# Blurring the three border rows on GpSimd as a stencil in the last loop of a convolution, GroupNorm and blur kernel

## The reference

```python
def _L1_conv_ref(input, kernel):
    PAD0, PAD1 = (2, 1)
    k = jnp.flip(kernel, (0, 1))
    w = jnp.broadcast_to(k[None, None], (c, 1) + k.shape)
    xp = jnp.pad(input, ((0, 0), (0, 0), (PAD0, PAD1), (PAD0, PAD1)))
    return lax.conv_general_dilated(xp, w, window_strides=(1, 1), padding='VALID', ...)
...
x = x + _L1_conv_ref(_gn(x), L1_conv_kernel)
```

## Time and profile before

| what | value |
|---|---|
| median of 3 runs | 5608.24 us (5605.93 to 5615.25) |
| profiled execution | 5612.93 us, of it a span of 5611.1 us |
| TensorE busy | 5223.0 us (93%) |
| VectorE busy | 4318.1 us (77%) |
| ScalarE busy | 3702.3 us (66%) |
| GpSimd busy | 2095.5 us (37%) |
| moved | 1729.80 MB, 308 GB/s in the mean |

### The profile page before, as it was taken

How to read it: one execution, slowest core, us unless ns; L and a number is a source line. 1 busy time by engine, 2 the same in 40 slices (tenths; PEclk the granted TensorE clock), 3 DMA queues, 4 the chain that set the end, 5 groups by cost and what they waited for, 6 DMA issues and landing times. The chain is left out here.

```text
span 5611.1 us, 67501 instructions
## 1 busy us (share of the span) xinstructions
PE 5223.0 (93%) x18280; PEld 3171.0 (57%) x18280; DVE 4318.1 (77%) x5293; ACT 3702.3 (66%) x4976; POOL 2095.5 (37%) x1393
## 2 busy tenths in 40 slices
PE   2888888899999999997699999999999999999999
PEld 1333333334555555563266666666666667667777
DVE  8555555418999999966988888888888888888833
ACT  0333333346777777756788788787887878878754
POOL 0000000017777777742333333333333333333354
PEclk9999999999999999999899999999999999999999
DMA  9999999942333333326999999999999999999986
GB/s 372 367 383 387 376 382 377 354 147 81 106 107 108 106 109 107 105 87 258 382 388 403 394 404 399 394 404 390 395 399 388 404 392 395 404 382 404 394 273 221
DMA packets 829589, 1729.80 MB, mean 308 GB/s; under 512 B 50064, under 2 KB 587152, under 8 KB 718608
## 3 DMA queue, kind: packets, MB, share of 16 engines
q1 hardware_dynamic: 485136, 1121.34, 53.8%
q10 hardware_dynamic: 344064, 604.05, 28.1%
HBM read 1050.95 MB, written 674.23 MB: 307 GB/s over the span
## 5 line engine op out<-in xcount | busy, mean ns | idle before, releaser
L1159 POOL TENSOR_TENSOR y_lo<-y_centred_tile,y_hi 128x1024 fp32r<-128x1024 f32 x512 | 1039.7, 2052 | 1721.1 <-ACT y_centred_tile L1509 1405.3
L1380 PE MATMUL blur_psum<-y_hi,band_hi 128*128 128x512 f32 x4096 | 1128.9, 417 | 8.8 <-DVE y_tile L1248 7.4
L1380 PE MATMUL blur_psum<-y_lo,band_hi 128*128 128x512 f32 x4096 | 1042.5, 396 | 7.5 <-POOL y_lo L1159 7.1
L1363 PE MATMUL conv_psum<-u_in,w_conv 128*128 128x512 f32 x2048 | 958.1, 610 | 84.2 <-DMA u_in<-u_scratch 36.1
L1380 PEld LDWEIGHTS blur_psum<-y_hi,band_hi 128*128 128x128 f32 x4096 | 765.8, 188 | 278.9 <-issue 100.6
L1380 PEld LDWEIGHTS blur_psum<-y_lo,band_hi 128*128 128x128 f32 x4096 | 769.7, 188 | 200.8 <-POOL y_lo L1159 16.5
L1220 DVE TENSOR_TENSOR pair_sums<-gelu_out,conv_psum 128x512 f32<-128x512 f32 x960 | 613.9, 683 | 308.3 <-ACT conv_psum L1471 308.0
L1248 DVE SCALAR_TENSOR_TENSOR y_tile<-blur_psum,rstd_all,y_tile 128x1024 f32<-128x1024 f32 x512 | 639.5, 1276 | 159.7 <-PE blur_psum L1380 152.2
L1471 ACT ACTIVATE gelu_out<-conv_psum,bn_shift,bn_scale 128x512 f32<-128x512 f32 x512 | 397.9, 777 | 522.0 <-PE conv_psum L1363 498.9
L1363 PEld LDWEIGHTS conv_psum<-u_in,w_conv 128*128 128x128 f32 x2048 | 393.8, 195 | 525.3 <-issue 384.2
L396 PE MATMUL z_psum<-x_resident,w_folded 128*128 128x512 f32 x1280 | 600.0, 624 | 28.0 <-ACT z_psum L425 19.1
(11 more groups left out here) (175 smaller groups left out, 5661.9 us busy)
## 6 DMA issues: line engine op xcount, KB each, us to landing
x_tile<-x SPq DMA_DIRECT2D x256, 1024.0 KB, 9.1
y_scratch<-x_tile ACTq DMA_DIRECT2D x256, 1024.0 KB, 7.7
y_tile<-y_scratch SPq DMA_DIRECT2D x512, 512.0 KB, 12.5
out<-y_tile ACTq DMA_DIRECT2D x512, 512.0 KB, 9.7
x_stream<-x SPq DMA_DIRECT2D x192, 1024.0 KB, 11.6
x_resident<-x SPq DMA_DIRECT2D x160, 1024.0 KB, 11.2
z_scratch<-z_tile ACTq DMA_DIRECT2D x256, 256.0 KB, 7.2
z_in<-z_scratch SPq DMA_DIRECT2D x256, 256.0 KB, 3.0
```

The lines of the kernel that those rows point to most:

```text
L1159: nc.gpsimd.tensor_tensor(y_lo[:, h, part, 2:2 + W], y_c[:, part, :], y_hi[:, h, part, 2:2 + W].bitcast(F32), ALU.subtract).then_inc(s_lo, 1)
L1363: nc.tensor.matmul(cv[s][:], w[:, s * C:(s + 1) * C], u_t[:, k % US, :], start=True, stop=True).then_inc(s_mm, 1)
L1380: ins = nc.tensor.matmul(bl[t][:, 2 * c:2 * c + 2, :], wt[:, kw, :], y[:, h, ch:ch + 2, kw:kw + W], start=(m == 0 and kw == 0), stop=(m == ...
```

## The change

The seam leaves TensorE and VectorE. GpSimd computes it as a stencil in fp32 from 112 partitions: 48 of them (16 channels x 3 rows) hold the left half of the columns, 48 more, from partition 64 on, the right half. Each partition gets the four rows that its output row needs, side by side in its free dimension (4 x 131), so that the row direction too is a sum along the free dimension. SP therefore issues eight loads for a quad (four rows for two column halves) and two stores, where it issued two loads and one store. ScalarE subtracts the mean in place (two instructions of 48 partitions). GpSimd then does four quarters, one behind each y_lo pair: column tap j times the window, added up, and in the last quarter the four rows are added together, scaled by the rstd, and the row itself is added. Each instruction waits for the one before it. SP's loads of a quad now wait until the stencil of the quad two before is done. The conv product no longer waits for the seam; the matrices of the seam and their products go, and the mean and rstd tables of the seam come from one product in place of two.

The diff, without the removed constants, bands and counts:

```diff
@@ SP, in load_group @@
-                    sp.wait_ge(s_sc, b * NQ - NQ + q + 1)
-                    sp.dma_start(seam_t[:, q % 2, :], yr[bass.ds(n * GRP, 16), 125:131, :]).then_inc(s_sin[q % 2], 16)
-
-                    sp.wait_ge(s_sst[q % KS], b * (16 * NQ // KS) - 16 * NQ // KS + 16 * (q // KS) + 16)
-                    sp.dma_start(keep_t[:, q % KS, :], yr[bass.ds(n * GRP, 16), 127:130, :]).then_inc(s_sin[q % 2], 16)
+                    sp.wait_ge(s_sdn, b * NQ - NQ + q + 1)
+                    for half, (to, cols) in enumerate(SEAM_PARTS):
+                        for kh in range(4):
+                            sp.dma_start(seam_t[64 * half:64 * half + 48, q % 2, kh, to],
+                                         yr[bass.ds(n * GRP, 16), 125 + kh:128 + kh, cols]).then_inc(s_sin[q % 2], 16)
@@ GpSimd @@
-                if g % QUAD == 2:
-                    pool.wait_ge(s_sc, b * NQ - NQ + g // QUAD + 3)
-                    nc.gpsimd.tensor_tensor(seam_lo[:, 2:2 + W], seam_c[:],
-                                            seam_hi[:, 2:2 + W].bitcast(F32), ALU.subtract).then_inc(s_slo, 1)
+
+            def seam_quarter(b, phase, k):
+                qq, j = divmod(k - LAG_QUARTER, QUAD)
...
+                taps = KR[0:SEAM_P, :].rearrange("p (a b) -> p a b", b=4)[:, :, j:j + 1].broadcast_to([SEAM_P, 4, SEAM_W])
+                window = y[:, :, j:j + SEAM_W]
+                if j == 0:
+                    pool.wait_ge(s_sc, 2 * at + 2)
...
+                    nc.gpsimd.tensor_tensor(seam_acc[:], window, taps, ALU.mult).then_inc(s_slk, 1)
+                    return
+                pool.wait_ge(s_slk, links + 2 * j - 1)
+                nc.gpsimd.tensor_tensor(seam_prod[:], window, taps, ALU.mult).then_inc(s_slk, 1)
+                pool.wait_ge(s_slk, links + 2 * j)
+                nc.gpsimd.tensor_tensor(seam_acc[:], seam_acc[:], seam_prod[:], ALU.add).then_inc(s_slk, 1)
+                if j < 3:
+                    return
+                pool.wait_ge(s_slk, links + 7)
+                nc.gpsimd.tensor_tensor(seam_acc[:, 0:2], seam_acc[:, 0:2], seam_acc[:, 2:4], ALU.add).then_inc(s_slk, 1)
+                pool.wait_ge(s_slk, links + 8)
+                nc.gpsimd.tensor_tensor(seam_acc[:, 0], seam_acc[:, 0], seam_acc[:, 1], ALU.add).then_inc(s_slk, 1)
...
+                nc.gpsimd.tensor_tensor(seam_o[:, slot, :], seam_acc[:, 0], scale, ALU.mult).then_inc(s_slk, 1)
+                pool.wait_ge(s_slk, links + 10)
+                nc.gpsimd.tensor_tensor(seam_o[:, slot, :], seam_o[:, slot, :], mean, ALU.subtract).then_inc(s_slk, 1)
+                pool.wait_ge(s_slk, links + 11)
+                nc.gpsimd.tensor_tensor(seam_o[:, slot, :], seam_o[:, slot, :], y[:, 2, 2:2 + SEAM_W],
+                                        ALU.add).then_inc(s_sdn, 1)
@@ TensorE @@
-                        if blurring and (k - LAG_BLUR) % QUAD == QUAD - 1:
-                            seam(b, phase, k, seam_products)
@@ VectorE @@
-                        if (k - LAG_BLUR) % QUAD == QUAD - 1:
-                            take_seam(b, k)
@@ ScalarE, in split_seam @@
-                nc.scalar.activation(seam_hi[:, 2:2 + W], seam_t[:, q % 2, :], ACT.Identity,
-                                     bias=nm_s[:, bass.ds(at, 1)]).then_inc(s_shi, 1)
-                nc.scalar.activation(seam_c[:], seam_t[:, q % 2, :], ACT.Identity,
-                                     bias=nm_s[:, bass.ds(at, 1)]).then_inc(s_sc, 1)
+                for half, (inside, _) in enumerate(SEAM_PARTS):
+                    part = seam_t[64 * half:64 * half + 48, q % 2, :, inside]
+                    nc.scalar.activation(part, part, ACT.Identity,
+                                         bias=nm_s[64 * half:64 * half + 48, bass.ds(at, 1)]).then_inc(s_sc, 1)
```

More of the change, by code:

```diff
@@ L52, in shape_constants @@
         k[:, K_TM + kh * 128:K_TM + (kh + 1) * 128] = p[:, None] - p[None, :] == kh - 2
[L53 to L59 removed]
+    for half in range(2):
+        m = np.arange(48)
+        k[:, K_SEAM + 64 * half:K_SEAM + 64 * half + 48] = p[:, None] % 16 == m[None, :] // 3
     k[:, K_QM:K_QM + C // 16] = p[:, None] // 16 == np.arange(C // 16)[None, :]
@@ L941 @@
 YS = 8
-KS = 4
+KS = 2
+SEAM_P = 112
+SEAM_W = W // 2
 AHEAD3 = 2
@@ L948 @@
 LAG_SEAM = AHEAD3 + LAG_BLUR + 3
+LAG_QUARTER = LAG_SPLIT + 2
+LINKS_SEAM = 11
 PADW = W + 4
@@ L1167, in body @@
             def body(b, phase):
-                for k in range(LAG_SPLIT if phase == END else UNITS):
+                for k in range(LAG_QUARTER if phase == END else UNITS):
                     if phase == FIRST:
@@ L1384, in blur @@
                 ins.then_inc(s_t, 1)
-            def seam(b, phase, k, products):
-                q = (k - LAG_BLUR) // QUAD
-                at = b * NQ - NQ + q
-                pe.wait_ge(s_shi, at + 1)
-                pe.wait_ge(s_slo, at + 1)
-                if phase <= MIDDLE:
-                    pe.wait_ge(s_ge, b * (4 * UNITS) + 4 * k + 3 + 4)
-                elif k == LAG_BLUR - 1 and phase == DRAIN:
-                    pe.wait_ge(s_tab, b)
-                if k != LAG_BLUR + QUAD - 1 or phase != SECOND:
-                    pe.wait_ge(s_sev, at)
-                for m, (wt, y) in enumerate(products):
-                    for kw in range(4):
-                        ins = nc.tensor.matmul(small[0:48, 0:W], wt[:, kw, :], y[:, kw:kw + W],
-                                               start=(m == 0 and kw == 0),
-                                               stop=(m == len(products) - 1 and kw == 3))
-                ins.then_inc(s_smm, 1)
             def gn2_average(b, phase):
```

120 lines of the change are left out of this document (50 added, 70 removed).

## The result

The changed kernel takes **5641.91 us** (median of 5 runs, 5626.83 to 5646.33) against 5608.24; the ratio is 1.0054, 95% interval 1.0043 to 1.0064. It is slower by 0.5%. The forecast was 5586, on the other side. The profiled execution is the shortest of its five (5626.83 us, span 5625.0), so I use its trace to find places and the medians to weigh them.

The account below looks back on a forecast made before the run. The prediction took TensorE to set the pace, with the GpSimd-VectorE shared inputs and the DMA close behind. From the profiled 5612.9 us, -52 + 22 + 7 gave 5590; the median, 4.7 us lower, gave 5586, range 5563 to 5645.

Parts of the forecast that it names:

- TensorE, -52 us: Last loop: eight seam products, 0.95 us per four units, leave TensorE in 55 groups where it sets the pace; -52 us.
- the 8.5 us at its start: Time around each batch's start, beside eight groups of four units; late y_lo was to be won back in it.
- The stencil's own price, 10.8 us and 0.6 for its waits: GpSimd's twelve stencil instructions per four units: 10.8 us, plus 0.6 for each waiting on the one before.
- The turns, 44.2 us for four units against a cover of 3.8: GpSimd and VectorE alternate on shared SBUF inputs: 44.2 us per four units; 3.8 us of y_lo lateness hidden; next to nothing lost.
- The rival in which the turns become the bound: GpSimd pays in full for VectorE's two-input work, from about 45.3 us per four units; slower, likelier 5635 us; chance 0.28.
- DMA, +22 us: More, smaller seam transfers make four units of traffic 45.1 us, later than TensorE asks: 3.1 us a batch, 22 in seven.
- SyncE at nothing: SP's wait for the stencil two groups back and its eight issues were costed at nothing, hidden by 13 us of cover.
- the same 13 us of cover: Loads are issued over two units ahead and y_tile lands in 13.9 us, so some 13 us of lateness are hidden.
- My 5 to 13 us for the eight: Time SP needs to issue the eight seam loads, at 585 ns least and 1686 median each: 5 to 13 us.
- The tail, +5: Last stretch: the last stencil quarter, 4.8 us, in GpSimd's gap of 4.17 costs 0.6 us eight times; 5 us.
- the end, +2: Behind the last y_lo, three stencil quarters, 10 us, replace a seam, blur products and an eviction; 2 us allowed.

Follow-up runs that it names:

- two loads: The changed kernel with two of the eight seam loads per quad, the stencil's instructions kept at full size: 5607.8 us, -1.6 against the kernel before.
- The trial with one product: The kernel before with one seam product per quad in place of eight, everything else kept: 5587.8 us, ratio 0.9963.
- the kernel with 2 columns: The changed kernel with each stencil instruction on 2 of its 256 columns, all loads, stores and waits kept: 5617.3 us, ratio 1.0010.
- four slots: The changed kernel with four slots of the seam tile in place of two, so SyncE waits for the stencil of four quads back: 5640.5 us, ratio 1.0054.
- one product and narrow loads: The kernel before with one seam product in place of eight and its two seam loads cut to 16 of 256 columns: 5585.4 us, ratio 0.9953.

## Why the prediction was wrong, step by step

*TensorE, -52 us.* The 0.95 us are gone from each quad, as said (43.65), and with two loads the ordinary units give all of it (38.6 us in six batches). But a batch was taken to get shorter by 8 x 0.95, with the 8.5 us at its start kept. **This is the first step that failed**: the start was costed as unchanged. In the changed kernel the starts of six batches are 31.9 us longer. TensorE waits there for u_in (12.8 us), for VectorE behind the statistics chain and for y_lo, and it runs at half clock for 44.4 us in place of 13.7. These 31.9 us are more than the forecast's whole gain of 22. The trial with one product, -21.7 us for 46, misses its share at the same places, but by a second gap that the changed kernel doesn't have; it is no measure of this loss. The row of the gap was there in the kernel before (2.54 us, "issue"), and I had not looked at it.

*The stencil's own price, 10.8 us and 0.6 for its waits.* Right: alone, four products at 1.05, three sums at 1.30 and the five small ones come to 4.2 + 3.9 + 2.5 = 10.6 us. Its mean in place is higher, 14.9, since that holds the turns.

*The turns, 44.2 us for four units against a cover of 3.8.* Right for the ordinary units, where they cost nothing: 43.65 us with the turns in it. Wrong for the start, in whose 8.5 us their lateness was to be won back. There they cost more, 15 us in six batches by the kernel with 2 columns against after (457.0 to 472.3), and 24 by the one with two loads against before. What I missed is the small VectorE instructions of the statistics chain, which take turns too (4.33 us for one element); the rows of before had one of 1.77 us. The rival in which the turns become the bound gave nearly the measured time (5635), by luck: the kernel with two loads, all turns in it, is at 5607.8.

*DMA, +22 us, and SyncE at nothing.* Together they measure 29.5 us, so the sum of the two is near, and the split is wrong. I had asked only how many bytes and pieces the engines move. The issues cost more: two in place of eight, or the burst split in two, gives 18 us or more back. **The second step that failed is "SP costed at nothing"**: I gave it "the same 13 us of cover" as the DMA term, but as I read it the cover is one, it was already spent there, and the eight issues lie ahead of the next unit's loads. My 5 to 13 us for the eight were right (9.2 to 12.1). Taking away the part that I feared, SyncE's wait for the stencil, changed nothing in the whole (four slots); it moved 20 us from the ordinary units to the starts. In the ordinary units of the changed kernel the loads take back 26.5 of the 38.6 us (1667.7 against 1641.2).

*The tail, +5, and the end, +2.* 11.5 us. I put the last quarter at the sum of its durations, 4.8, and left out its share of the waits between instructions, 0.5, which I had myself added for the whole stencil. In a gap of 4.17 that makes 1.15 in place of 0.6, and the end took the rest.

Put together by the differences of whole kernels: -21.7 + 29.5 + 20.0 + 6 = +33.7, where the forecast had -52 + 22 + 7 = -23. These are differences between kernels and not the sizes of causes: the -21.7 holds the trial kernel's own second gap, and the other two are measured against it. By place, the two traces have -38.6 for the products and +26.5 for the loads in the ordinary units, +31.9 at the starts, -5.0 in what is left of the middle and +11.5 in the tail; that is the 26.3 us that this execution lost there.

## What to carry to other kernels

Time taken off an engine inside a loop's pass arrives only if the place where one pass hands over to the next gets no longer. Look at that place first, and weigh it apart from the ordinary units. Look at TensorE's granted clock there too: a gap was paid for twice here, once as itself and once by the half clock behind it. A trial with the work taken out can have gaps of its own; compare where its time went, and not its total alone. Count a change's transfers by number and by what stands behind them in their queue, not by bytes alone; a cover may be spent once. When work is dealt out in slices, no slice, waits included, may be longer than the smallest gap on the engine that takes it.

## What the runs showed of the hardware

- How long an issue holds its engine varies: 0.34 us for x_tile before, 6.92 in the changed kernel, and up to 7.12 for two on ScalarE, with ScalarE's own work behind it. That the queue was backed up is my reading; no run measures it.
- GpSimd's instructions of 112 partitions alone: 0.40 to 0.47 us for 128 elements, 0.74 for 256, 1.05 (product) and 1.30 (sum) for 512. While VectorE reads two inputs from SBUF, one of 128 took 1.33 and 2.24 us. The Trainium skill, "GPSIMD Engine Reference", section "8. Key points", names this contention; the trace agrees, and adds that it falls on tiny instructions of both engines with the length of the other's: 4.33 us for a VectorE instruction of one element per partition.
- Where the loop's pass changes, TensorE stood idle for 2.2 to 2.5 us at five places of the kernel before, waiting for nothing that the profile names. With one product and narrow loads a second gap of 3.1 to 3.8 us stood behind the first; the changed kernel has none. All fifteen gaps ended 2.5 to 2.7 us after a 16 KB packet on the queue q8 "instruction". That this is the cause is not tested.
- In the kernels before and after TensorE's granted clock was full (2.4 GHz) in the ordinary units and half (1.2 GHz) in stretches near the batches' starts, in the kernel before each at the end of a gap of 2.2 to 2.6 us: 13.7 us in all before, 44.4 in the changed kernel, 71.7 with four slots. Eight conv products, most of them in such a stretch, took 5.23 us, and 3.60 elsewhere.
